# Layer 0: queries turned by transposing DMAs, not identity matmuls; ScalarE, not GpSimd, writes the high part of the own keys' probabilities

## The reference, cut to what matters

```python
q  = _ln(_fp8_linear_pertensor(ln_out, wq, ...).reshape(b, s, g, hpg, d), qln_w, qln_b)      # own queries
k  = _ln(_fp8_linear_pertensor(ln_out, wk, ...).reshape(b, s, g, d), kln_w, kln_b)           # own keys
v  = _fp8_linear_pertensor(ln_out, wv, ...)
core = _gqa(q, k, v)                       # softmax over the 256 own tokens
qx = _ln(_fp8_linear_pertensor(ln_out, wqx, ...).reshape(b, s, g, hpg, d), qxln_w, qxln_b)   # queries for the context
kvx = jnp.einsum('bsi,oi->bso', cond, w_kv_x)
kx = _ln(kx.reshape(b, sc, g, d), kxln_w, kxln_b)
xout = _gqa(qx, kx, vx)                    # softmax over the 1601 context tokens
catq = _div_clamp_fp8(jnp.concatenate([core, xout], axis=-1), proj_smooth)
return jnp.einsum('bsi,oi->bso', catq, wproj) * (proj_in_scale * proj_w_scale)
```

## Time and profile before

| | |
|---|---|
| time, median of 3 runs | 1680.82 us (1679.46 to 1682.97) |
| span of the profiled execution | 1678.0 us |
| TensorE busy | 1597.7 us, 95% |
| VectorE, ScalarE busy | 1389.4 and 1387.6 us, 83% each |
| GpSimd busy | 1130.8 us, 67% |
| large transfers' queue | 604464 packets, 258.05 MB |

### The profile page before, as it was taken

The page is one execution under the profiler, slowest core; times in us unless marked ns, Lnnn a source line. Parts: engine busy times, 40 slices in busy tenths (PEclk is TensorE's granted clock), DMA queues, the critical chain, the costliest instruction groups (busy, mean ns, idle before and its releaser), DMA issues. The chain is left out here.

```text
span 1678.0 us, 44059 instructions
## 1 busy us (share of the span) xinstructions
PE 1597.7 (95%) x15996; PEld 1003.1 (60%) x15996; DVE 1389.4 (83%) x3489; ACT 1387.6 (83%) x2340; POOL 1130.8 (67%) x1766
## 2 busy tenths in 40 slices
PE   3799999999999999999999999997898999999998
PEld 1476777767777677777777777765564333333333
DVE  7889999999999989999988999999896755655422
ACT  6688888888887888888887887876347999999997
POOL 3568778687787877888787878875575655646300
PEclk9799999999999999999999999998999999999999
DMA  5299989899989998999999999999323222222100
GB/s 179 85 200 204 195 196 198 188 203 208 211 193 202 223 206 187 213 223 220 206 198 215 220 220 192 201 189 237 95 48 115 46 46 74 45 40 46 33 14 14
DMA packets 608904, 261.11 MB, mean 156 GB/s; under 512 B 576560, under 2 KB 581680, under 8 KB 607280
## 3 DMA queue, kind: packets, MB, share of 16 engines
q1 hardware_dynamic: 604464, 258.05, 71.3%
q10 hardware_dynamic: 4224, 0.25, 0.2%
HBM read 99.15 MB, written 17.29 MB: 69 GB/s over the span
## 5 line engine op out<-in xcount | busy, mean ns | idle before, releaser
L1810 PE MATMUL score<-KK,QT 128*128 128x512 bf16 (+2 forms) x1920 | 341.8, 322 | 7.4 <-DVE mxp L1289 7.3
L1830 PE MATMUL pv<-PT,VV 128*128 128x256 bf16 (+1 forms) x2880 | 335.7, 273 | 6.1 <-DMA PT<-PB 6.1
L1565 ACT ACTIVATE PB<-S,rsum 128x1024 bf16<-128x1024 f32 (+1 forms) x256 | 246.3, 988 | 105.5 <-DVE rsum L1320 79.6
L1830 PEld LDWEIGHTS pv<-PT,VV 128*128 128x128 bf16 (+1 forms) x2880 | 278.3, 98 | 70.8 <-issue 31.6
L1311 DVE SCALAR_TENSOR_TENSOR PB<-S,rsum,PB 128x1024 bf16<-128x1024 f32 (+1 forms) x256 | 291.1, 1138 | 0.0
L1810 PEld LDWEIGHTS score<-KK,QT 128*128 128x128 bf16 x1920 | 157.9, 98 | 145.3 <-DVE mxp L1289 14.5
L1555 ACT ACTIVATE S<-S,nmx 128x1601 f32<-128x1601 f32 x128 | 210.1, 1641 | 3.6 <-DVE nmx L1301 3.5
L2870 ACT ACTIVATE P<-score 128x1024 f32<-128x1024 f32 x196 | 198.0, 1054 | 1.7 <-PE score L2962 0.8
L1689 PE MATMUL tb<-stage,wsb 128*128 128x512 bf16 (+1 forms) x768 | 149.5, 337 | 5.2 <-DVE stage L643 3.9
L2982 PE MATMUL pv<-P,V 128*9 128x256 f32 (+1 forms) x2288 | 152.2, 380 | 1.1 <-DVE pv L2253 0.8
L1125 POOL TENSOR_SCALAR S<-S,rsum 128x256 f32<-128x256 f32 x128 | 72.2, 564 | 115.3 <-DVE rsum L1320 107.4
(11 more groups left out here) (293 smaller groups left out, 3679.6 us busy)
## 6 DMA issues: line engine op xcount, KB each, us to landing
x<-rs_d SPq DMA_DIRECT2D x16, 936.0 KB, 5.0
rsb<-rs_d SPq DMA_DIRECT2D x16, 936.0 KB, 5.6
wsb<-w_split SPq DMA_DIRECT2D x46, 256.0 KB, 4.7
wsb<-w_split SPq DMA_DIRECT2D x23, 512.0 KB, 4.8
wpr<-in_wprojT SPq DMA_DIRECT2D x23, 512.0 KB, 6.5
context_d<-stage SPq DMA_DIRECT2D x16, 400.2 KB, 3.8
l_ctx<-context_d SPq DMA_DIRECT2D x4, 1601.0 KB, 7.8
rawh<-in_w_all SPq DMA_DIRECT2D x12, 512.0 KB, 5.8
```

What stands on the lines that cost most here:

```text
L1565: e.activation(m.PB[n % 2][:, 2 * a:a + b], m.S32[n % 2][:, a:b], ACT.Copy, scale=m.rsum[n % 2][:, 1:2]).then_inc(s["p_hi"], 1)
L1810: i = e.matmul(m.score[:, at:at + b - a], qt[:, kind, qp, q * P:(q + 1) * P], kk[:, kp, a:b], start=(k == 0), stop=(k == 2))
L1830: i = e.matmul(m.pv[:, at:at + 256], vv[0:rows, v, t, :], m.PT[k % 2][0:rows, turned(c, a), :], start=(c == first and r == 0), stop=(c == ...
```

## The change

The queries keep their tokens on partitions until they are finished. Weight and bias, which stand along the columns in this layout, come as a row that is laid out on all partitions (`qrow`). GpSimd multiplies and adds it (`query_weighted`), ScalarE writes the high part (`query_high`), GpSimd the low part (`query_low`), both into a tile `q16` of 128x1024 bf16. One transposing DMA on SP's queue (`turn_q`) turns all eight 128x128 tiles into `QT`. The slots `TQ0` and `TQ1` are empty, and the eight f32 matmuls of a block are gone. `kn` is one buffer where there were two, and so is `q16`.

For the own keys' probabilities, ScalarE writes the high part from the unscaled exponentials behind `p_hi` of the second half; GpSimd does the scaling in place and the difference, and waits for ScalarE's signal `s_hi` where it waited for `sum_read`.

```diff
-            m.kn = [sb(c, f"kn{i}", [P, 512], F32) for i in range(2)]
-            m.t32 = sb(c, "t32", [P, 512], F32)
+            m.kn = sb(c, "kn", [P, NQ, D], F32)
+            m.qrow = sb(c, "qrow", [P, 4, D], F32)
+            m.q16 = sb(c, "q16", [P, 2, NQ * D], BF16)
...
-SLOTS = (("Q0",), ("K0",), ("K1",), ("TQ0",), ("K2",), ("K3",), ("Q1",), ("SS",), ("V0",), (), ("V1",), ("TQ1",), ("V2",),
-         ("V3",), ("PR",))
+SLOTS = (("Q0",), ("K0",), ("K1",), (), ("K2",), ("K3",), ("Q1",), ("SS",), ("V0",), (), ("V1",), (), ("V2",), ("V3",),
+         ("PR",))
...
+    def turn_q(it, i):
+        if not it < NGB:
+            return
+        e.wait_ge(s["q_lo"], 2 * it + i + 1)
+        if it >= 2:
+            e.wait_ge(s["bank_full"], 8 * (it - 1))
+        e.dma_start_transpose(m.QT[it % 2][:, 1 - i, :, :].rearrange("p a (k q) -> p (a k) q", q=P),
+                              flat(m.q16[:, :, :])).then_inc(s["qt_in"], 16)
...
+        turn_q(it + 1, 0)
         turn_p(4 * it, 1)
...
         if it == NGB - 1:
             load_projection(NGB - 1)
+        turn_q(it + 1, 1)
         turn_p(4 * it + 1, 1)
...
+    def query_weighted(it, i):
+        if not it < NGB:
+            return
+        c, w = 2 * it + i, 2 * (1 - i)
+        if c == 0:
+            e.wait_ge(s["const_in"], 80)
+        e.wait_ge(s["normed"], c + 1)
+        e.tensor_tensor(m.kn[:, :, :], m.kn[:, :, :], m.qrow[:, w:w + 1, :].broadcast_to([P, NQ, D]),
+                        ALU.mult).then_inc(s["q_t32"], 1)
+        e.wait_ge(s["q_t32"], 2 * c + 1)
+        e.tensor_tensor(m.kn[:, :, :], m.kn[:, :, :], m.qrow[:, w + 1:w + 2, :].broadcast_to([P, NQ, D]),
+                        ALU.add).then_inc(s["q_t32"], 1)
...
-        e.tensor_copy(m.QT[it % 2][:, kind, 0, :], m.t32[:, :]).then_inc(s["q_hi"], 1)
         e.wait_ge(s["q_hi"], c + 1)
-        e.tensor_tensor(m.QT[it % 2][:, kind, 1, :], m.t32[:, :], m.QT[it % 2][:, kind, 0, :],
-                        ALU.subtract).then_inc(s["q_lo"], 1)
+        e.tensor_tensor(m.q16[:, 1, :], flat(m.kn[:, :, :]), m.q16[:, 0, :], ALU.subtract).then_inc(s["q_lo"], 1)
...
-        e.wait_ge(s["sum_read"], n + 1)
-        if n >= 2:
-            e.wait_ge(s[f"pt1_in{n % 2}"], 16 * (n // 2))
-        e.tensor_scalar(p, p, m.rsum[n % 2][:, 0:1], 1.0, ALU.mult, ALU.mult).then_inc(s["s_hi"], 1)
-        e.wait_ge(s["s_hi"], 2 * n + 1)
-        e.tensor_copy(hi, p).then_inc(s["s_hi"], 1)
-        e.wait_ge(s["s_hi"], 2 * n + 2)
+        e.wait_ge(s["s_hi"], n + 1)
+        e.tensor_scalar(p, p, m.rsum[n % 2][:, 0:1], 1.0, ALU.mult, ALU.mult).then_inc(s["s_lo"], 1)
+        e.wait_ge(s["s_lo"], 2 * n + 1)
         e.tensor_tensor(lo, p, hi, ALU.subtract).then_inc(s["s_lo"], 1)
...
+    def query_high(it, i):
...
+        c = 2 * it + i
+        e.wait_ge(s["q_t32"], 2 * c + 2)
         if c:
-            e.wait_ge(s["q_lo"], c)
-        e.activation(m.t32[:, :], bank_of(m, f"TQ{i}")[:, :], ACT.Identity, scale=dcol(m, w + "_w"),
-                     bias=dcol(m, w + "_b")).then_inc(s["q_t32"], 1)
+            e.wait_ge(s["qt_in"], 16 * c)
+        e.copy(m.q16[:, 0, :], flat(m.kn[:, :, :])).then_inc(s["q_hi"], 1)
...
+        if h:
+            e.activation(m.PB[n % 2][:, 2 * a + XEND:a + PCOLS], m.S32[n % 2][:, SELFC:PCOLS], ACT.Copy,
+                         scale=m.rsum[n % 2][:, 0:1]).then_inc(s["s_hi"], 1)
...
-    def turn_queries(it, i):
...
-        for k in range(NQ):
-            r = e.transpose(bank[:, k * P:(k + 1) * P], m.kn[i][:, k * D:(k + 1) * D], m.ident[:, :])
-        r.then_inc(s["pa_full"], 1)
...
-            e.wait_ge(s["q_lo"], 2 * it + 1 + half)
+            e.wait_ge(s["qt_in"], 16 * (2 * it + 1 + half))
```

More of the change, by code:

```diff
@@ L76 @@
 pa_full k_sq k_bias k_lo sums_out sums_in kr_pow v_hi v_lo st_done mv_done rs_pow nm_done normed
-q_hi q_t32 q_lo pw_in pw_last pw_hi pw_lo acc_done
-bank_full mm negmax exp_s sum_read p_pad p_hi p_lo s_hi s_lo
+q_t32 q_hi q_lo qt_in pw_in pw_last pw_hi pw_lo acc_done
+bank_full mm negmax exp_s sum_read set_zero p_hi p_lo s_hi s_lo
 pt0_in0 pt0_in1 pt1_in0 pt1_in1 tv_done pv_free clipped y_exp y_mag y_add yq_done
@@ L804, in act_prologue @@
 def act_prologue(e, m, s):
-    e.wait_ge(s["const_in"], 64)
+    e.wait_ge(s["const_in"], 80)
     at = SCAL.index("gx0")
@@ L938, in wait_bank @@
         it, at = it - 1, at + len(SLOTS)
-    if not SLOTS[at] or SLOTS[at] == ("PR",) and 0 <= it < LAG:
+    while not SLOTS[at] or SLOTS[at] == ("PR",) and 0 <= it < LAG:
         at -= 3
@@ L947, in wait_bank @@
         e.wait_ge(s["k_lo"], 4 * it + int(before[1]) + 1)
-    elif before[0] == "T":
-        e.wait_ge(s["q_t32"], 2 * it + int(before[2]) + 1)
     elif before == "SS":
@@ L1157, in pool_attention @@
         split_self(4 * it - 1)
+        query_weighted(it + 1, 0)
         if it < NGB - 1:
@@ L1172, in pool_attention @@
         split_self(4 * it + 1)
+        query_weighted(it + 1, 1)
         key_norm(it + 1)
@@ L1708, in squares @@
         if it == 0:
-            e.wait_ge(s["p_pad"], 1)
+            e.wait_ge(s["set_zero"], 2)
         for j in range(SQG):
@@ L1765, in queries @@
         r.then_inc(s["pa_full"], 1)
-    def turn_queries(it, i):
-        if not it < NGB:
-            return
-        bank = bank_of(m, f"TQ{i}")
-        wait_bank(e, s, it, f"TQ{i}")
-        e.wait_ge(s["normed"], 2 * it + i + 1)
-        for k in range(NQ):
-            r = e.transpose(bank[:, k * P:(k + 1) * P], m.kn[i][:, k * D:(k + 1) * D], m.ident[:, :])
-        r.then_inc(s["pa_full"], 1)
     def project(i):
@@ L2113, in dve_router @@
     elif stage == 1:
-        e.wait_ge(s["rank_done"], 1)
+        e.wait_ge(s["set_zero"], 1)
         find("oh")
@@ L3112, in layout @@
     out["dcols"] = np.ascontiguousarray(np.stack([l0(n) for n in DCOLS], axis=1))
+    out["qrow"] = np.concatenate([l0(n) for n in ("qln_w", "qln_b", "qxln_w", "qxln_b")])
     out["scal"] = np.concatenate([z.reshape(-1) for z in (
```

50 lines of the change are left out of this document (21 added, 29 removed).

## The result

The changed kernel takes 1862.03 us (median of 4 runs, 1860.53 to 1864.78), beside 1680.16 before: 1.108 times as long, 95% interval 1.106 to 1.109. The sign was forecast; the size is 182 us where 70 were, and outside the range. The page of the kernel after: engines with their busy time and share, and TensorE's granted clock in 40 slices.

What follows compares the result with a forecast made beforehand. TensorE was taken as the bound before; afterwards late own queries set the period, 36.9 or 35.5 us: +35.7, +26.1, about -1 gave +61, 1742 us; clock +9 made 1751, stated as 1750. Range 1662 to 1795.

Steps and rivals of the forecast that it cites:

- The hole ahead of the second half of scores, ended by the own queries: Sign on TensorE's timeline: a 2 to 4 us wait before a second half of scores, ended by `DMA QT<-q`.
- the signs of the power and of the block's length: Keys' row power starts 3.5 to 4.5 us later; blocks near 37 us from 17 on, nearly 36 before.
- step 3: Path of the next pair's own queries, through ScalarE, GpSimd and SP: 36.9 us a block with weights ahead, 35.5 without.
- Step 2: GpSimd loses three casts' worth, gains two 1.19 us instructions per query tensor; ScalarE gains 1.2 us a block; all hidden as work.
- 18.6 us from one second half of scores to the end of `V0`: First term of the own queries' path, from TensorE's timeline before: 19.0 us, less one turn group, unchanged otherwise.
- As mere work, all this is hidden: Work added on GpSimd and ScalarE fits their idle time (ScalarE 1.2 in 5.8 us a block); only its order costs.
- step 4: Turn of the context queries, due before the first half of scores with SP free: costs nothing.
- The clock: TensorE's waits of 3.7 us drop its clock in a quarter of the blocks, 1.7 us each: +9 us.
- 0.40 us copy: ScalarE's new copy of 128x256 f32 to bf16 per tile; GpSimd waits for it, within a 1.75 us term.
- step 6: ScalarE waits for the sum before casting `V2`, delaying the exponentials behind it 1.9 us, which falls into the 36.9 us period.
- the forecast chain: Second half of scores to the next, with weights ahead: 18.6 + 1.75 + 1.3 + 2.5 + 2.8 + 2.2 + 7.8 = 36.9 us.

Runs made afterwards that it cites:

- the clock held up: Changed kernel plus nine 512-column matmuls, their result overwritten, in every second half of scores of a first tile, ahead of the wait for own queries: 1858 us, ratio 1.104.
- the copy early: Changed kernel with ScalarE's copy of the own columns moved ahead of the first half's high part, for tile 4it+1 alone: 1785 us, ratio 1.062.
- both repairs: Changed kernel with the own-column copy of tile 4it+1 moved ahead and product and sum on 2 of 512 columns for both queries: 1753 us, ratio 1.041.

## Why the prediction was right, and where it was wrong

- *The hole ahead of the second half of scores, ended by the own queries:* right. 30 of them, 3.1 us in the mean, 3.7 forecast. The own queries land 7.0 us after issue (median; 6 to 8 forecast). Blocks last 40.6 us from 17 on and 39.7 before that, where 37 and nearly 36 were the sign: the difference is right, the level is not. The power starts 6.2 us later in the block, not 3.5 to 4.5. It is the signs of the power and of the block's length that failed.
- *The late links (step 3):* right in place and nearly in size. Scaling and difference 1.2 (forecast 1.3), power 2.7 (2.8), landing of the own queries 8.0 behind the start of the row's read (7.8; the earlier trace rows). Product and sum took 3.0, not 2.5: one took about what I had taken from the earlier trace rows, 1.23, the other 1.73, behind a difference of VectorE. The row's write landed after 1.4 us, not 2.2. (Step 2 counts the casts that GpSimd loses as three; the edit takes four of 128x256 and two of 128x512. No term of the sum hangs on it.)
- *18.6 us from one second half of scores to the end of `V0`, "with the first half as it was":* the step that failed. In block 27 it took 1167.93 - 1147.44 = 20.5 us, and the copy ended another 2.8 us later, not 1.75, because ScalarE was still at the norm of the own queries (`kn`, until 1169.09) when `V0` was done. Together that is 2.9 us late, 3.4 in the mean over 28 blocks. The other links nearly cancel (+0.5, -0.8, +0.2), and 36.9 + 2.9 = 39.8 is the measured period of that block; 31 times 2.9 is 90 of the 111 us by which the forecast missed. I took it from TensorE's timeline before, as TensorE's own work. The chain of waits shows that it goes over VectorE's clip, exponent step and `rsum` to ScalarE. In block 27, 1.3 us of it stand where TensorE's clock was low and 1.1 where VectorE waited for GpSimd; but with the clock held up only 0.4 us was left of it at the copy, while without GpSimd's products the copy came 2.2 us earlier. "As mere work, all this is hidden", I wrote of the added work, because GpSimd had idle time; its price was on VectorE, which had 2 us a block.
- *The turn of the context queries, "Nothing"* (step 4): wrong. Alone it costs 39 us; inside the change the products of it cost 31.
- *The clock:* forecast 5 falls of 3.4 us, +9 us. It stood at the lower level for 117 us of the 1210, in 23 stretches, far more; but holding it up gave 4 us. Its size was wrong, and so was the reasoning that "since 18.6 us of the chain is its own work, so does the period".
- *The own keys' part:* its 0.40 us copy and later split were in the sum. That they are in VectorE's way in all four tiles of a block was not.
- *Why 33 + 77 became 182:* with the queries' part the late sum holds ScalarE ahead of `V2` (step 6 had 1.9 us), and the own copy that starts the sum is itself ScalarE's. With the copy early the parts nearly add: 21 and 77 make 98, and 104 were measured, so that this one place takes all but 6 of the 72 away. For the products (105) the same can't be told, since the queries' part wasn't run without them. That the 72 need both parts is what the runs show; how they split over VectorE and the order is open.
- *What stays below:* without the products the kernel stands at 1757, and with both repairs at 1753. The period of 36.7 to 36.9 there is what the forecast chain gave for the whole change, 36.9. But it is reached without the products' 2.5 us, and it is held by the moment at which SP comes to the turn of the own queries (29.5 us into the block), which is no term of the forecast. So it agrees by chance.

## What to carry to other kernels

Before moving work to an engine with idle time, look at which other engine its instructions hold up, and how full that one is: here 2.6 us of GpSimd work a block, without a reader, cost VectorE 1.7 us and the kernel 1.5%. Don't take a stretch of the path as one engine's constant because that engine is busy in it; follow the chain of waits through it. And where two engines feed each other in written orders, the place of the shortest instruction can be worth more than any duration: try it one tile at a time.
